# Latent attention and FP4 feed-forward on one core: attention's results stored undivided, denominators inverted in pairs of groups, keys and queries stored unsplit, weight pieces quantized in two parts

## What is computed

```python
# attention, on x = layernorm(input): D_MODEL, HEADS = 512, 16; D_H = 32; D_HR = 16; latent width 128
c_q, c_kv = x @ W_DQ, x @ W_DKV
Qc, Kc, V = c_q @ W_UQ, c_kv @ W_UK, c_kv @ W_UV          # 16 heads of 32
Qr, Kr = rope(c_q @ W_QR), rope(x @ W_KR)                 # 16 heads of 16; one Kr for all heads
scores = clip(concat(Qc, Qr) @ concat(Kc, Kr).T, -80, 80) # causal
attn = softmax(scores / sqrt(48)) @ V
x = input + attn @ W_O
# feed-forward, on y = layernorm(x); quant = blockwise FP4 quantize and dequantize
gate, up = quant(y) @ quant(w_gate).T, quant(y) @ quant(w_up).T
out = x + quant(silu(gate) * up) @ quant(w_down).T
```

## Time and profile before

| | |
|---|---|
| Runs | 3178.27 us median of 3 (3177.66 to 3180.22) |
| Profiled execution: its time, its span | 3176.54 us, 3174.7 us |
| TensorE busy | 3028.5 us (95%) |
| VectorE busy | 2666.9 us (84%) |
| ScalarE, GpSimd busy | 1225.3 us (39%), 656.9 us (21%) |
| Mean granted TensorE clock | 0.989 of full |
| DMA in part one, two, three | about 340, 170, 30 GB/s |
| Last matmul of part one, first score of part two | 375, 414 us after the start |
| First turned block of part three | 1400 us |

### The profile page before, as it was taken

How to read it: one execution, slowest core, us unless ns; L and a number is a source line. 1 busy time by engine, 2 the same in 40 slices (tenths; PEclk the granted TensorE clock), 3 DMA queues, 4 the chain that set the end, 5 groups by cost and what they waited for, 6 DMA issues and landing times.

```text
span 3174.7 us, 65118 instructions
## 1 busy us (share of the span) xinstructions
PE 3028.5 (95%) x23276; PEld 2222.8 (70%) x23276; DVE 2666.9 (84%) x4496; ACT 1225.3 (39%) x1833; POOL 656.9 (21%) x632
## 2 busy tenths in 40 slices
PE   7999779999999999989999999999999999999999
PEld 6777634444444444447888888888888888888887
DVE  6777559999999999888888888888888888888886
ACT  3544346666666666652222222222222222222221
POOL 2434300000000000002223323332332232222332
PEclk9999889999999999989999999999999999999999
DMA  6999956665766666651000000000000000000000
GB/s 231 333 341 337 317 163 168 167 182 160 185 174 161 190 163 177 178 169 37 30 31 30 30 30 30 30 30 24 30 27 30 30 30 30 30 30 30 30 24 14
DMA packets 234571, 351.90 MB, mean 111 GB/s; under 512 B 17616, under 2 KB 117840, under 8 KB 234448
## 3 DMA queue, kind: packets, MB, share of 16 engines
q1 hardware_dynamic: 234448, 350.59, 36.3%
HBM read 205.55 MB, written 144.97 MB: 110 GB/s over the span
## 4 chain that ended last, share of the span: by engine, by line
PE 54%; DVE 1%; ACT 0%; issue 0%; POOL 0%; DVEq 0%
PE p_ring L1566 19%; PE p_ring L1594 15%; PE ps_od L1566 11%; PE ps_od L1546 5%; PE p_ring L1584 2%; PE p_ring L1574 1%; DVE sb_wg_lo L1462 0%; PE ps_od L1594 0%; PE p_ring L1546 0%; PE p_ring L1609 0%; DVE sb_fp_tmp L102 0%; DVE sb_wd_lo L1462 0%; DVE sb_h_amax L88 0%; DVE sb_stage L1433 0%; DVE sb_ht_lo L1451 0%
## 5 line engine op out<-in xcount | busy, mean ns | idle before, releaser
L788 ACT ACTIVATE sb_probs<-scores 128x1024 f32<-128x1024 f32 (+3 forms) x768 | 585.8, 812 | 348.9 <-PE scores L988 342.9
L847 DVE TENSOR_SCALAR sb_probs<-sb_probs 128x2048 f32<-128x2048 f32 (+3 forms) x320 | 289.1, 903 | 84.4 <-ACT sb_probs L788 81.3
L1003 PE MATMUL ps_od<-sb_probs,sb_v 128*32 128x512 f32 (+3 forms) x3072 | 328.2, 499 | 11.7 <-DVE sb_probs L847 7.2
L1264 POOL TENSOR_TENSOR sb_stage<-sb_stage,sb_h_inv 128x512 f32<-128x512 f32 (+1 forms) x192 | 210.3, 1095 | 544.4 <-DVE sb_h_inv L94 544.4
L988 PEld LDWEIGHTS scores<-sb_q_hi,sb_k_hi 32*128 32x128 f32 x1536 | 73.8, 182 | 338.7 <-ACT sb_probs L788 273.0
L1566 PE MATMUL p_ring<-sb_wg_hi,sb_xq_hi 128*128 128x512 f32 (+1 forms) x1024 | 295.3, 369 | 0.3 <-DVE sb_wd_lo L1462 0.3
L1566 PE MATMUL p_ring<-sb_wg_lo,sb_xq_hi 128*128 128x512 f32 (+1 forms) x1024 | 290.5, 365 | 0.0
L1566 PE MATMUL p_ring<-sb_wg_hi,sb_xq_lo 128*128 128x512 f32 (+1 forms) x1024 | 289.9, 364 | 0.0
L1594 PE MATMUL p_ring<-sb_wd_hi,sb_ht_hi 128*128 128x512 f32 x693 | 275.9, 398 | 0.0
L1594 PE MATMUL p_ring<-sb_wd_hi,sb_ht_lo 128*128 128x512 f32 x693 | 270.2, 390 | 0.0
L1594 PE MATMUL p_ring<-sb_wd_lo,sb_ht_hi 128*128 128x512 f32 x693 | 269.8, 389 | 0.0
(11 more groups left out here) (183 smaller groups left out, 6685.7 us busy)
## 6 DMA issues: line engine op xcount, KB each, us to landing
kq<-sb_kq_out SPq DMA_DIRECT2D x64, 1024.0 KB, 8.6
sb_xin<-in_L_attn_x_dram SPq DMA_DIRECT2D x32, 512.0 KB, 5.9
rq<-sb_r_out SPq DMA_DIRECT2D x32, 512.0 KB, 6.8
v<-sb_v_out SPq DMA_DIRECT2D x64, 256.0 KB, 6.0
sb_k_hi<-kq SPq DMA_DIRECT2D x32, 512.0 KB
sb_q_hi<-kq SPq DMA_DIRECT2D x32, 512.0 KB
sb_k_lo<-kq SPq DMA_DIRECT2D x32, 512.0 KB
sb_q_lo<-kq SPq DMA_DIRECT2D x32, 512.0 KB
```

What stands on the lines that cost most here:

```text
L788: act.activation(probs[:, k % PROBS, 2 * pair:2 * pair + 2, off:BANK], scores[(2 * k + pair) % RING2][:, :, off:BANK], ACT.Exp, scale=SCAL ...
L847: i = dve.tensor_scalar(pr, pr, P_MAX, P_MIN, ALU.min, ALU.max)
L1003: mm = pe.matmul(ps_o[rows, off:BANK], v_sb[s][:, j, rows], probs[:, k % PROBS, i, off:BANK], start=(j == 0), stop=last)
L1264: pool.tensor_tensor(x, x, spread(h_inv[:, a // QB:b // QB], (b - a) // QB), ALU.mult).then_inc(h_y, 1)
```

## The change

- **Part one.** K and Q leave PSUM in one plain copy by ScalarE, are stored once, and ScalarE itself frees their slots (and V's) on a semaphore of its own; VectorE has no work on them. C becomes two units of one bank. The rope weights are ordered by even and odd columns, so that R is one unit instead of two: VectorE multiplies two 128x1024 forms, GpSimd adds and subtracts 128x1024. `row_stats` and the deviation look one half further ahead and stand after R. Sixteen of the 32 weight pieces are quantized here, one a half, wholly on VectorE (ten instructions) behind X1.
- **Part two.** Per group VectorE no longer turns, inverts, turns back and multiplies; ScalarE copies `ps_d` out (`copy_denominators`, at k = 0 and k = 5), SP stores four rows of it in `dn`. Once per two groups SP loads a 128x64 chunk of denominators, VectorE inverts it (k = 9 of s = 1), SP stores it in `dinv`. Keys and queries are loaded whole (two loads of 512 KB instead of four) and split here: ScalarE rounds at k = 1 and 2, VectorE subtracts at k = 3 and 4. The remaining 16 pieces take two groups each; ScalarE's product by a constant moves from k = 6 to k = 11 of s = 0, and it waits there for VectorE's scaling at the same k.
- **Part three.** For each tile SP issues four more loads (the inverse denominators of 16 heads, each read 32 times over), behind the store of an earlier result, and GpSimd multiplies `at_in` by them (`divide_tile`, 128x512) ahead of its first hidden slice. `PREP_SLOTS` is 7. The last half group's denominators go out through DRAM, and VectorE inverts the last chunk before its first tile's body.

```diff
-UNITS1 = ["C", "KR", "X0", "X1", "K0", "K1", "Q0", "Q1", "R0", "R1", "V0", "V1"]
+UNITS1 = ["C0", "C1", "KR", "X0", "X1", "K0", "K1", "Q0", "Q1", "R", "V0", "V1"]
...
-                for k, name in enumerate(("KR", "R0", "R1")):
+                for k, name in enumerate(("KR", "R")):
...
+                    (freed_last if last else freed)(pool, n, name)
+                    pool.tensor_tensor(a, a, b_, ALU.add).then_inc(rope_sum, 1)
+                    if name == "R" and not is_last(b):
+                        inverse_deviation(n + 2)
+
+                    pool.wait_ge(rope_hi, n * 2 + k + 1)
+                    pool.tensor_tensor(lo, a, hi, ALU.subtract).then_inc(rope_lo, 1)
...
-                        act.copy(kq_out[:, half, k, 0, 2 * m:2 * m + 2, :].bitcast(F32R), ps[:]).then_inc(act_hi, 1)
+                        act.copy(kq_out[:, half, k, 2 * m:2 * m + 2, :], ps[:]).then_inc(act_free, 1)
...
+                    if name == ("KR" if last else "X1"):
+
+                        dve.wait_ge(piece_loaded, n * 16 + 16)
+                        fp4_scales(dve, piece_in[:], piece_amax[:], piece_scale[:], piece_inv[:], piece_scaled,
+                                   n * SCALES_STEPS)
...
+    def divide_tile(self, pool, i, inverses, loads):
+
+        pool.wait_ge(self.in_loaded[i], loads)
+        pool.wait_ge(self.inv_loaded, inverses)
+        at = self.at_in[:, i]
+        pool.tensor_tensor(at, at, self.inv_in[:], ALU.mult).then_inc(self.at_divided, 1)
...
+            def copy_denominators(it2, s, half):
+
+                act.wait_ge(pv_done, step_no(it2, s, NS if half else 4) + PROBS)
+                act.wait_ge(d_stored[1 - half], it2 * 32 + (s * 16 + 16 + 16 * half))
+                act.copy(d_sb[:], ps_d).then_inc(d_free, 1)
...
-                    if k == 6:
-                        act.wait_ge(w_y, it2 * 2 + (s + 1))
-                        act.mul(w_big[:], w_sb[:, s, :], MAGIC).then_inc(w_magic, 1)
+                    if k == 0 and not first:
+                        copy_denominators(*preceding(it2, s), 1)
+                    if k == 5:
+                        copy_denominators(it2, s, 0)
+                    if k in (1, 2) and not last:
+                        round_raw(*following(it2, s), k - 1)
+                    if k == 11 and s == 0:
+                        act.wait_ge(w_y, it2 + 1)
+                        act.mul(w_big[:], w_sb[:], MAGIC).then_inc(w_magic, 1)
...
+                    elif k == 11 and s == 0:
+                        own(dve, w_scaled, scaled + 4)
+                        dve.wait_ge(w_stored, it2 * 16 + 16)
+                        dve.tensor_tensor(w, blocks_of(w_in[:]), spread(w_inv[:], WP // QB), ALU.mult).then_inc(w_y, 1)
...
-PREP_SLOTS = 8
+PREP_SLOTS = 7
...
             sp.wait_ge(ps_free, number(0, -1, "WO") + RING3 + 1)
-            sp.wait_ge(last_stored, 16)
+            sp.wait_ge(last_stored, 32)
+            ahead.load_chunk(sp, 2 * B - 1)
             ahead.load_tile(sp, 0, 2)
...
+            dve.wait_ge(ahead.chunk_loaded, 16 * 2 * B)
+            ahead.invert_chunk(dve)
```

More of the change, by code:

```diff
@@ L403, in body @@
                 his = [u for u in HI1 if u in units]
-                if not last:
-                    row_stats(n + 1)
-                dve.wait_ge(stored[half], b * STORES1 + STORES1)
                 for name in units:
@@ L475, in body @@
                 units = units_of(last)
-                his = [u for u in HI1 if u in units]
-                for name in units:
-                    number = unit(n, units.index(name))
+                for place, name in enumerate(units):
+                    number = unit(n, place)
                     ps = ring[slot(units, name)]
+                    if place >= RING1:
+                        before = units[place - RING1]
+                        (freed_last if last and before in FREED_BY_DVE else freed)(pe, n, before)
+                    else:
+                        freed(pe, n - 1, UNITS1[place - RING1])
                     if name[0] == "X":
@@ L630, in attention @@
         w_inv = sb("w_inv", [P, WP // QB])
-        w_loaded = [sem(f"w_loaded{s}") for s in range(2)]
+        w_loaded = sem("w_loaded2")
         w_scaled = sem("w_scaled")
@@ L727, in body @@
                 if not first:
-                    before = (it2, 0) if s == 1 else (it2 - 1, 1)
-                    store_piece(*before)
                     if not last:
@@ L733, in body @@
                         load(*following(it2, s))
-                    store(*before, 1)
+                    store(*preceding(it2, s), 1)
+                if s == 1 and not (isinstance(it2, int) and it2 == 0):
+                    sp.wait_ge(ahead.chunk_stored, it2 * 16 + 16)
+                    for h in range(HALF):
+                        sp.wait_ge(d_stored[h], it2 * 32 + 16)
+                    ahead.load_chunk(sp, it2 - 1)
+                if not (isinstance(it2, int) and it2 == G2 - 1):
+                    load_raw(it2 + 1, s)
                 if last:
@@ L763, in _ @@
                                pattern=[[1, P]], channel_multiplier=-1).then_inc(s_cst, 1)
+            ahead.divide_tile(pool, 0, 16 * NI, 32)
         @block.scalar
@@ L768, in _, with round_raw @@
             act.sem_inc(o_free, 1)
+            act.sem_inc(d_free, 1)
+            act.sem_inc(ahead.chunk_stored, 32)
+            def round_raw(it2, s, k):
+                act.wait_ge(raw_loaded, it2 * 64 + (s * 32 + 32))
+                act.copy((k_hi, q_hi)[k][s][:], kq_raw[:, k]).then_inc(raw_rounded, 1)
             for h in range(HALF):
                 act.sem_inc(at_stored[h], 16)
-            for h in range(2):
-                act.sem_inc(w_stored[h], 16)
+                act.sem_inc(d_stored[h], 16)
+            act.sem_inc(w_stored, 16)
             def exponentials(it2, s, k, first, between=None):
@@ L917, in body @@
                                           ALU.max).then_inc(w_scaled, 1)
-                    elif k == 2:
-                        if not first:
-                            normalise(*before, 1)
+                    elif k == 1:
+                        own(dve, w_rounded, rounded + 1)
+                        dve.scalar_tensor_tensor(out=w_tmp[:], in0=w_big[:], scalar=1.5, in1=w_sb[:], op0=ALU.max,
+                                                 op1=ALU.add).then_inc(w_rounded, 1)
+                    elif k == 2 and s == 0:
@@ L946, in body @@
                     elif k == 9:
                         add_sums(it2, s, 0)
-                        own(dve, w_rounded, rounded + 1)
-                        dve.scalar_tensor_tensor(out=w_tmp[:], in0=w_big[:], scalar=1.5, in1=w_all, op0=ALU.max,
-                                                 op1=ALU.add).then_inc(w_rounded, 1)
+                        if s == 1 and not (isinstance(it2, int) and it2 == 0):
+                            dve.wait_ge(ahead.chunk_loaded, it2 * 16)
+                            ahead.invert_chunk(dve)
@@ L956, in body @@
                     elif k == 11:
-                        if not last:
-                            turn(it2, s, 1)
                         own(dve, w_rounded, rounded + 3)
```

456 lines of the change are left out of this document (257 added, 199 removed).

## The result

The changed kernel takes **3398.26 us** (median of 4, 3396.96 to 3399.97) against 3177.97 before on the same chip: 1.0693 times as long, 95% interval 1.068 to 1.0707. The forecast was 3175, with a range that ended at 3205. It is slower by 220 us, and nearly all of it was lost in part two.

A forecast was written before the change was run, and what follows sets the result against it. It took TensorE to bound parts one and three, and the score, exponential, score loop part two. Start −0.5, part one −16, first seam −6, part two +14, first tile +5 sum to −3.5: 3175 us, range 3150 to 3205.

The forecast's parts named there:

- the denominators' store: Part two, rival: ScalarE's copy at k = 5 waits for the previous copy's store; +31, 3206 us; chance 0.12.
- the seam: From part two to three: +5 for the first tile; an idle TensorE's lower clock could add to this.
- Part two otherwise: Part two's sum: +26.4 for the wait at k = 11, −9 and −3 of relief, together +14; bounds −15 to +30.
- the wait at k = 11: Part two: ScalarE's product waits for VectorE's scaling, `score` of step 2 is 1.65 us late once in two groups: +26.4.
- the relief: Part two: work leaving VectorE shortens the waits for clip, −9; fewer key and query loads shorten v's wait, −3.
- Part one: VectorE's circle, including `normalise` held by GpSimd's rest, sets a half at 21.0 us: −16; bounds −30 to −5.
- The first rival: Part one goes at TensorE's pace: a half takes 20.1 us, −30 instead of −16, 3161 us; chance 0.14.
- The first seam: Between parts one and two: fewer bytes in flight shorten the barrier and land v sooner, −6; between −2 and −10.
- Behind part two: First tile of part three: VectorE's residual waits for the last chunk, starting at 1435.0 instead of 1429.22: +5.8.
- Part three: GpSimd's division fits its idle time and VectorE absorbs holds: cost 0; rival of VectorE held, +45, 3220 us, chance 0.04.

The follow-up runs named there:

- two buffers: Changed kernel with a denominator buffer (`d_sb`) for each half of the queries, so a copy waits for the store of a whole group earlier: 3182.62 us, 1.0022 of before.

## Why the prediction was wrong, step by step

**The step that failed** is the wait of ScalarE's copy for the denominators' store. The sum has no term for it (it costs the copies "at nothing"); it stands only as a rival, "the denominators' store", with a chance of 0.12. That rival's mechanism, place and direction were right; how it judged its own condition, and its price, were not. It said that ScalarE would wait if issue and landing together exceeded 12.7 us, took 8.0 for the landing, and then did not add the issue, though the trace of the kernel before had it. In the kernel before, SyncE's row of these loads is

```profile
913.97 3.88 SPq L695 DMA_DIRECT2D sb_qr<-rq  x8
918.03 0.67 SPq L695 DMA_DIRECT2D sb_kr_hi<-kr  x1
918.90 0.62 SPq L695 DMA_DIRECT2D sb_kr_lo<-kr  x1
919.71 0.41 SPq L708 DMA_DIRECT2D sb_v<-v  x1
```

6.15 us for the eleven loads. With 0.65 for the result's store ahead of the denominators' (that trace has 1.30 for two at 895.97, and up to 8.1 elsewhere) and 8.0 for the landing that is 14.8 against 12.7, a wait of 2 us as the likely case and not one with a chance of 0.12. Measured were 8.3 and 10.9 us in one group, 6.2 and 10.1 in the other, against 12.3 and 13.9 between the starts of the two copies (the second lengthened by the low clock behind k = 11). The landing of 8.0 was a median over all stores of results, which in that trace took from 2.0 to 14.0 us. "About 1.0 us × 31" was therefore too low by a factor of five (163.3 us in 30 waits), and there was no term for the lower clock of TensorE that follows, 59 us more, though the prediction named this danger for the seam and its own row showed it.

**The argument against it**, a DMA share of 0.63, was a mean over part two. It says nothing of a burst: in the changed kernel the share is 0.41 over part two and 0.98 where the store stands behind the loads.

**Part two otherwise** was right. With two buffers it takes 993.7 us, 13.0 more than before; the forecast was +14 with 1 off for its end. Of this the wait at k = 11 was put at 26.4 and measured 29.5 (2.24 us of ScalarE's wait, 1.84 a pair in the time); without it part two gains 17.4, where 13 was forecast, so the relief was worth 4 more. No cost of ScalarE's copies and roundings shows, as forecast.

**Part one** was right: a half takes 21.11 us (21.0 forecast), with TensorE waiting 0.90 (0.9). Before, a half took 22.14 us (turnings at 188.01 and 210.15); the 22.00 of the prediction is the width of the window in the earlier trace rows. The last matmul of part one comes 18.5 us sooner, where 16.5 were forecast; the stretch from the last turning on gives 2.9 of it (32.4 us before, 29.6 now), and the prediction had nothing for that. The rows of one half, which answer to the earlier trace rows:

```profile
217.50 1.02 POOL L300 TENSOR_TENSOR sb_rstd<-sb_vareps,sb_mhalf 128x4 f32<-128x4 f32 x1 [0.71 <-DVE sb_vareps L388]
218.49 2.41 POOL L320 TENSOR_TENSOR sb_r_out<-sb_turned,sb_r_out 128x1024 f32<-128x1024 f32 x1
...
219.59 2.95 DVE L396 TENSOR_SCALAR sb_xhat<-sb_xin,sb_moments,sb_rstd 128x512 f32<-128x512 f32 x4
...
221.69 2.01 PE L498 MATMUL p_ring<-sb_ident,sb_xhat 128*128 128x128 f32 x16 [0.90 <-DVE sb_xhat L396]
```

`normalise` takes 2.95 us where it took 1.91: it waits for GpSimd's rest to end. That the sum came out is in part luck: it let `normalise` start only when the rest was done, and left out the residual of C, which fills that time (1.29 us from 218.39 on). The Trainium skill ("SBUF — State Buffer", Who interferes with whom) exempts an instruction with one input in SBUF only outside VectorE's faster modes, and names `tensor_scalar` as one that can enter them and then be held by GpSimd. The trace agrees: the first of the four, which has one operand of full width, takes 1.58 us beside GpSimd's rest, against 0.53. The first rival (TensorE's pace, 20.1 us a half) did not come about, but its number was right: that is what a half takes once the hold and the queue behind it are gone, 20.07.

**The first seam** was wrong in size: −6 was forecast, and from the last matmul of part one (375.43 before, 356.90 after) to the first score it is 39.0 and 38.7 us, −0.3. Barrier and first v are 16.90 and 17.97 now, against 16.51 and 19.79 in the earlier trace rows, and the warm-up between them takes 3.47 us instead of 2.34, since the change also raises it from 20 to 32 products, which neither the section on the change nor the prediction mentions; it lies inside the wait for v, so it should cost nothing. From the barrier's end v is 0.7 us sooner, and the barrier itself ends 0.4 later: fewer bytes in flight did not shorten it.

**Behind part two** the chunk cost what was forecast, +6.6 against +5.8. It is issued at 1640.44, and VectorE's residual starts 40.0 us behind the last product with ones (1604.64), where the prediction's 1435.0 gives 39.8. VectorE's wait is 9.6 us and not about 5.

```profile
1644.17 0.55 DVE L666 RECIPROCAL sb_chunk<-sb_chunk 128x64 f32<-128x64 f32 x1 [9.61 <-DMA sb_chunk<-dn]
1644.64 0.63 DVE L1531 TENSOR_TENSOR sb_x<-p_ring,sb_x_in 128x512 f32<-128x512 f32 x1
```

**Part three** was costed at 0 and lost 6.2, not by GpSimd's division, which stays in the kernels that have the 6.2 back, but by the loads that feed it.

Of the 3398 us, then, 216 are the store's place, 29 the scaling at k = 11, and about 25 the hold and the queue in part one, the chunk and the inverses; what the change gains without them is 48 us, 1.5% of the kernel before. The order of two of SyncE's lines alone hid most of it.

## What to carry to other kernels

A buffer that is written, stored and written again has a loop of its own: add up the copy, what the issuing queue has in front of the store, and the landing behind the bytes already issued, and compare the sum with the time between two writes. Take each term from the row that stands at that place, not from a median or a mean share, and if the sum is near the period, put the store first or give it a second buffer. Where TensorE waits for several microseconds, add what its matmuls then cost at half the clock, there and at the shorter waits that follow; and where a wait is put on one engine to relieve another, look at what is queued behind everything that waits for it in turn.

## What the hardware showed

- TensorE's granted clock fell to 0.50 during and behind a wait of 7.45 us, and again, 14 us after it had risen, behind one of 1.91 us; the same 1.91 us leave it at 1.00 in the kernel without the long waits. The same 13052 matmul records took 59 us more with ScalarE's waits of 3.0 and 7.45 us in a pair of groups, and 54.5 more with about 1.6 and 4.5.
- A store of 8 KB took 10.1 and 10.9 us to land with some 2 MB of loads issued just ahead of it, and 8.6 and 7.7 us with a quarter of a megabyte less. SyncE's issue of a 256 KB store there took 1.65 to 1.83 us, and 0.38 with 0.9 MB less.
- VectorE's instruction behind a loop's branch sat idle 25.8 us in 13 waits when four loads of 64 KB were issued 2 us ahead of two others, and 3.2 in 3 when they were issued 3 us behind them.
